# Experts run only on the rows routed to them, in gathered blocks of 128, and gelu by ScalarE's own function

## The chip, the cores and the metric

One core of a Trainium2 chip runs the whole program. The metric is the device time of one execution in microseconds (us). Engines: PE is TensorE, DVE is VectorE, ACT is ScalarE, POOL is GpSimd, SP is SyncE, which only issues DMAs here.

## The reference

x is 16 sequences of 128 rows (the 16 "tiles") with 256 columns. Four stages follow one another, each on a layernorm of x and each added back to x:

- A: attention with 32 query heads of 8 columns over 8 key/value heads, keys and values straight from ctx (128 x 64).
- B: mixture of experts. Each row gets eight sigmoid scores and its two best of 8 experts:

```python
scores = sigmoid(xf @ gate_w.T)
_, sel = top_k(scores + expert_bias, 2)
rin = xf[tok_idx] * sc_sorted[:, None]
for e in range(8):
    h = silu(rin @ w1[e].T) * (rin @ w3[e].T)      # 256 -> 128
    out_sorted += (sorted_exp == e) * (h @ w2[e].T)  # 128 -> 256
routed = zeros.at[tok_idx].add(out_sorted)
shared = (silu(xf @ sw1.T) * (xf @ sw3.T)) @ sw2.T
```

- C: causal attention with 16 heads of 16 columns and projections Wq, Wkv, Wout.
- D: a two-layer network (256 to 1024 to 256) whose weights are rounded to -1, 0, 1 and whose activations are rounded to 8 bits per row, with the tanh form of gelu between the layers.

## The kernel before

Work is cut into parts named by stage and number, and done once for each tile: "B3/5" is part B3 of tile 5. For each engine `PROGRAMS` (lines 82 to 207) is a written list of such words, and `walk` issues them in just that order, so a part that waits holds everything behind it on its engine. Several tiles are under way in different stages at once. Parts hand over by semaphores; TensorE writes into a ring of 4 small (2 KB) and a ring of 2 big (4 KB) PSUM buffers, and a part that fills one first waits for the reader of the buffer's earlier use (`fill`).

Stage A per tile: A1 transposes the normalised tile, ScalarE copies it out, GpSimd splits it into three bf16 parts (`split`), SyncE stores these to DRAM and reads them back as stacked rows of QA (A1r). A2 makes scores once for their maximum (VectorE `neg_max`, line 1149), A3 carries the maximum back as two more rows, A4 makes the scores again transposed, ScalarE exponentiates them, A5 multiplies with the values, A6 transposes and scales. Stage C has the same shape, with projections in front and a causal mask by GpSimd (line 1052).

Stage B per tile: B1 transposes; B2 makes the shared expert and the gate scores; ScalarE takes the exp of the scores, VectorE ranks the eight experts of a row in some ten small operations (lines 1188 to 1206). B3 and B4 (lines 636 to 640) multiply the whole tile with the w1 and w3 of four experts each; ScalarE takes tanh per expert with the row's score as scale, VectorE multiplies (`products`, line 1213), and GpSimd multiplies with a coefficient that is zero for the six experts not chosen (`weigh`, line 1040). B5 transposes the nine hidden tiles, B6 (line 651) sums nine products with w2.

Stage D per tile: DX quantises, D1 transposes, D2 makes 1024 columns, VectorE scales them to z; then the gelu is made by hand: ScalarE squares z (line 908), VectorE (line 1254), ScalarE tanh (line 913), VectorE (line 1260). Its result is quantised (line 1136, 917, 1268), D3 transposes, D4 multiplies and GpSimd adds to x.

At the start SyncE loads the first tiles and the constant rows of KA and KC, whose semaphore `stacks_set` TensorE awaits before its first instruction; ScalarE issues all weight loads. K splits the keys of A in four chunks; SyncE reads each back into KA. S1 and S2 round the weights of D. rstd of every norm is a pow on GpSimd (line 977).

## Time and profile before

| | us |
|---|---|
| median of 3 runs | 653.4 (653.2 to 656.77) |
| the profiled execution's own time | 653.34 |
| its span in the profile | 651.6 |
| TensorE busy | 526.5 |
| VectorE busy | 455.4 |
| ScalarE busy | 296.3 |
| GpSimd busy | 290.8 |
| mean granted TensorE clock, share of full | 0.941 |

The profile is of one execution. The time outside the span is 1.7 us. "Busy" counts an engine's instructions, overlaps once; issuing a DMA, loading a register and waiting are not counted. A float32 product is recorded as two passes, so its group has twice as many entries as the code has calls. The tables hold the rows on which the later argument rests; a group of the view by line tells first the line, engine and operation, then what is written from what, the shapes, the number, and then busy time, mean duration in ns of one, and idle time in front of them with what ended it.

### The profile page before, as it was taken

What the parts mean: (1) busy time and instruction counts of PE and PEld (TensorE: products, weight loads), DVE (VectorE), ACT (ScalarE), POOL (GpSimd) and SP (SyncE); (2) the same over time, 40 slices, a digit from 0 to 9 for tenths busy, and PEclk for the clock granted to TensorE, in tenths of its full rate; (3) what the DMA queues carried; (4) which work ended last, traced back from release to release, by engine and by line L of the source; (5) the groups of instructions that cost most, each with busy time, mean ns of one, the idle gap of its engine ahead of it and who ended that gap; (6) DMA issues with size and microseconds to landing.
All of it is one profiled execution on the core that took longest, in us unless ns stands there. A gap on an engine that the chain in (4) does not pass through costs nothing.

```text
span 651.6 us, 11302 instructions
## 1 busy us (share of the span) xinstructions
PE 526.5 (81%) x3800; PEld 326.5 (50%) x3816; DVE 455.4 (70%) x929; ACT 296.3 (45%) x563; POOL 290.8 (45%) x516
## 2 busy tenths in 40 slices
PE   0035598799999999999999999999999999885651
PEld 0022254355656565656565656565656475564421
DVE  1017848666686878787888877787777777857763
ACT  0122143444446464646454545565555575344332
POOL 5462233445627363636363635353535354456210
PEclk9999788799999999999999998999898999998675
DMA  8642541313140404040404040504040303022000
GB/s 254 178 112 57 139 110 27 85 22 81 31 97 28 105 25 108 26 108 25 108 20 114 16 109 4 121 5 109 4 107 6 81 4 82 24 61 82 2 17 8
DMA packets 82105, 43.96 MB, mean 67 GB/s; under 512 B 48832, under 2 KB 77888, under 8 KB 82048
## 3 DMA queue, kind: packets, MB, share of 16 engines
q1 hardware_dynamic: 78336, 37.98, 23.8%
q10 hardware_dynamic: 3712, 5.26, 2.5%
q8 instruction: 31, 0.51, 0.3%
q14 instruction: 26, 0.21, 0.1%
HBM read 30.42 MB, written 12.32 MB: 66 GB/s over the span
## 4 chain that ended last, share of the span: by engine, by line
PE 56%; DVE 16%; POOL 10%; issue 8%; ACT 5%; DMA 3%; SPq 2%; POOLq 0%; ACTq 0%; DVEq 0%
PE big L625 17%; PE small L605 5%; PE small L562 3%; ACT PC L826 3%; PE big L593 3%; DVE neg_maxA L1149 3%; PE small L655 2%; PE small L613 2%; PE small L648 2%; POOL PC L1052 2%; POOL x L1030 2%; PE small L675 2%; PE big L578 2%; PE small L735 2%; PE small L766 2%
## 5 line engine op out<-in xcount | busy, mean ns | idle before, releaser
L1149 DVE TENSOR_REDUCE neg_maxA<-big 128x8 f32<-128x1024 f32 x64 | 76.7, 1214 | 19.9 <-PE big L578 19.9
L856 ACT ACTIVATE tB<-big,route_half 128x128 f32<-128x128 f32 x128 | 36.5, 368 | 93.2 <-PE big L625 93.2
L1044 POOL TENSOR_TENSOR vB<-vB,route_c 128x512 f32<-128x512 f32 x32 | 33.3, 1040 | 98.9 <-DVE vB L1217 98.9
L826 ACT ACTIVATE PA<-big 128x1024 f32<-128x1024 f32 x64 | 64.7, 1025 | 23.8 <-PE big L593 23.6
L625 PE MATMUL big<-w1T,xTB 128*128 128x512 f32 x128 | 64.6, 628 | 2.9 <-DVE vB L1210 2.7
L655 PE MATMUL small<-w2T,hTB 128*128 128x256 f32 x288 | 65.9, 383 | 0.6 <-ACT hTB L871 0.6
L1052 POOL TENSOR_SCALAR_AFFINE_SELECT PC<-PC 128x1024 f32<-128x1024 f32 x32 | 35.2, 1105 | 56.9 <-ACT PC L826 56.9
L625 PE MATMUL big<-w3T,xTB 128*128 128x512 f32 x128 | 60.5, 595 | 0.0
L655 PEld LDWEIGHTS small<-w2T,hTB 128*128 128x128 f32 x288 | 53.5, 190 | 7.8 <-ACT hTB L871 1.1
L826 ACT ACTIVATE PC<-big 128x1024 f32<-128x1024 f32 x32 | 32.4, 1024 | 21.9 <-PE big L707 21.9
L1175 DVE SCALAR_TENSOR_TENSOR tB<-tB,big 128x512 f32<-128x512 f32 (+1 forms) x48 | 26.4, 550 | 21.4 <-ACT tB L856 21.2
L625 PEld LDWEIGHTS big<-w3T,xTB 128*128 128x128 f32 x128 | 24.6, 193 | 31.3 <-issue 31.3
L1149 DVE TENSOR_REDUCE neg_maxC<-big 128x8 f32<-128x1024 f32 x32 | 38.1, 1216 | 2.2 <-PE big L692 2.1
L625 PEld LDWEIGHTS big<-w1T,xTB 128*128 128x128 f32 x128 | 22.7, 196 | 31.3 <-issue 17.2
L578 PE MATMUL big<-KA,QA 48*128 48x128 bf16 x512 | 26.0, 225 | 14.6 <-DMA QA<-parts_qA 9.1
L562 PE MATMUL small<-ident,xnA 128*128 128x128 f32 x32 | 8.2, 344 | 35.4 <-DMA KC<-onesb 21.8
L605 PE MATMUL small<-PA,VA 128*32 128x512 f32 x256 | 36.4, 653 | 0.0
L593 PE MATMUL big<-QA,KA 50*128 50x512 bf16 x128 | 25.1, 402 | 8.5 <-DVE neg_maxA L1149 3.9
L688 PE MATMUL big<-mask,identb 128*128 128x512 bf16 x64 | 26.5, 414 | 6.3 <-ACT PC L826 4.2
L838 ACT ACTIVATE OA<-small 128x512 f32<-128x512 f32 x32 | 19.1, 597 | 25.6 <-PE small L605 25.5
L578 PEld LDWEIGHTS big<-KA,QA 48*128 48x128 bf16 x512 | 15.2, 97 | 26.1 <-DMA QA<-parts_qA 10.5
L692 PE MATMUL big<-KC,QC 96*128 96x128 bf16 x256 | 27.1, 232 | 0.0
(171 smaller groups left out, 1213.7 us busy)
## 6 DMA issues: line engine op xcount, KB each, us to landing
parts_qA<-QP SPq DMA_DIRECT2D x16, 192.0 KB, 3.0
QA<-parts_qA SPq DMA_DIRECT2D x32, 96.0 KB
parts_kC<-KPC SPq DMA_DIRECT2D x16, 192.0 KB, 2.1
KC<-parts_kC SPq DMA_DIRECT2D x16, 192.0 KB, 3.1
parts_qC<-QPC SPq DMA_DIRECT2D x16, 192.0 KB, 2.4
QC<-parts_qC SPq DMA_DIRECT2D x16, 192.0 KB, 2.9
x<-in_x SPq DMA_DIRECT2D x16, 128.0 KB, 3.0
QA<-parts_qA SPq DMA_DIRECT2D x32, 64.0 KB
```

The source lines that it names most:

```text
L562: last = transpose(dst[:, c * P:(c + 1) * P], src[:, c * P:(c + 1) * P], idn[:])
L578: last = mm(ps[:, c * BANK + g * P:c * BANK + (g + 1) * P], QA[u][rows, G0 * j + g, :], KA[rows, j, t * P:(t + 1) * P], start=True, stop=True)
L593: last = mm(ps[:, c * BANK:(c + 1) * BANK], KA[rows, j, t * P:(t + 1) * P], QA[u][rows, G0 * j:G0 * (j + 1), :], start=True, stop=True)
L605: last = mm(ps[SLOT * j:SLOT * (j + 1), :], VA[u][:, kv, :], PA[:, kv * G0:(kv + 1) * G0, :], start=True, stop=True)
L625: last = mm(ps[:, o:o + n], xTB[:, c, :], w[c], start=(c == 0), stop=(c == DC - 1))
L655: last = mm(ps[:, 0:D], hTB[:, e, :], w_2[:, e, :], start=(e == 0), stop=(e == NE - 1))
L692: last = mm(ps[:, b * BANK + i * P:b * BANK + (i + 1) * P], QC[u][0:K1, h, :], KC[u][0:K1, h, :], start=False, stop=(i == 3))
L826: return op(dst[:, 8 * j:8 * (j + 1), :], ps[:].rearrange("p (h t) -> p h t", t=P), ACT.Exp, scale=scale).then_inc(S[name], 1)
L856: ins = op(tB[:, (e0 + i) * HID:(e0 + i + 1) * HID], ps[:, i * HID:(i + 1) * HID], ACT.Tanh, scale=rt["half"][:, e0 + i:e0 + i + 1])
L1044: g.tensor_tensor(hB[:, sl].rearrange("p (e h) -> p e h", e=4), vB[:, sl].rearrange("p (e h) -> p e h", e=4), rt["c"][:, e0:e0 + 4].unsque ...
L1052: g.affine_select(out=p, in_=p, compare_op=ALU.is_ge, fill=0.0, base=0, pattern=[[0, 8], [1, P]], channel_multiplier=-1).then_inc(S["PC_ca ...
L1149: v.tensor_reduce(dst[:, 8 * j:8 * (j + 1)], ps[:].rearrange("p (h t) -> p h t", t=P), FREE, ALU.max, negate=True).then_inc(S[name], 1)
```

## The change

The tiles are taken through stage B in batches of 4, 8 and 4. Each tile still goes through the shared expert and the gate (B1, B2, B5, B6), now with one product of 264 columns for both sides. BX stores its normalised rows to DRAM. For four tiles at a time R ranks the experts; R2 counts, by a product with a triangle of ones, how many rows before a row chose the same expert, which gives the place of each (row, choice) in a table sorted by expert. SC scatters the entries (row number, half score, half squared score) there by indirect DMA, two for each tile. `plan` works out where each block of 128 places begins and whose expert it is. A batch of n tiles has 2n + 7 blocks, so 15, 23 and 15, whatever the routing.

For a block, MB loads a register and 128 entries, MG gathers 128 rows of x by indirect DMA, M1 transposes them, M2 multiplies with w1 and w3 of the one expert whose column is in a register, M3 transposes the hidden tile, M4 multiplies with w2, MY stores 128 result rows. YG gathers the two result rows of each row by indirect DMA, and CY adds them to x. Buffers: 3 for gathered rows, 2 for each later step.

The gelu is one ScalarE activation (`Gelu_apprx_tanh`) from z to g2. D1's copy moves from VectorE to ScalarE. The first bf16 part of a split is written by ScalarE out of PSUM, and not by GpSimd. EPS is added by VectorE. The constant rows are awaited where they are used; the weights are issued in three portions, the later ones after the first KA and QA; the reads of KA move to ScalarE's queue; the rounding of the weights of D borrows PC, so that C6/0 waits for it. All five written orders are new; a stretch of TensorE's shows how blocks stand between parts of other tiles. The diff, cut:

```diff
-GROUPS = ((8, 1), (0, 4), (4, 4))
+BATCHES = ((0, 4), (4, 8), (12, 4))
+RT = 4
+MOST = max(n for _, n in BATCHES)
+NB = 2 * MOST + E - 1
+BLOCKS = tuple((2 * t0 + i * (E - 1), 2 * n + E - 1) for i, (t0, n) in enumerate(BATCHES))
...
+        M3/22 M3/23 D4/3 M2/24 M2/25 M4/22 M4/23 M1/26 M1/27 M3/24 M3/25 A5.0/13 M2/26 M2/27 M4/24 M4/25 M1/28 M1/29
...
+    rows_x = [nc.dram_tensor(f"rows_x{i}", (n * P, D), F32).ap() for i, (_, n) in enumerate(BATCHES)]
+    table = [nc.dram_tensor(f"table{i}", (places(n), 4), F32).ap() for i, (_, n) in enumerate(BATCHES)]
+    rows_y = [nc.dram_tensor(f"rows_y{i}", (n * P, D), F32).ap() for i, (_, n) in enumerate(BLOCKS)]
...
-            sp.wait_ge(S["onesb"], 1)
-            for c in range(2):
-                sp.dma_start(KA[c * HALF + K0:c * HALF + K0 + 2, :, :], onesb[:]).then_inc(S["stacks_set"], 16)
-            for x in KC:
-                sp.dma_start(x[K1:KM, :, :], onesb[0:2 * H1, :]).then_inc(S["stacks_set"], 16)
...
+                sp.wait_ge(S["zeros_set"], 1)
+                for x in table:
+                    sp.dma_start(x.rearrange("(p n) w -> p (n w)", p=P), zeros[:, 0:x.shape[0] * 4 // P]).then_inc(S["zeros_in"], 16)
...
+                i = block_of(b)[0]
+                n = BATCHES[i][1]
+                s.wait("plan", i)
+                sp.wait_ge(table_in[i], 16 * 2 * n)
+                if b >= NQ:
+                    sp.wait_ge(ent_in[b % NQ], 16 * (b // NQ))
+                place0 = sp.value_load(row_of[0:1, b:b + 1], min_val=0, max_val=places(n) - P)
+                sp.dma_start(entB[:, b, :], table[i][bass.ds(place0, P), :]).then_inc(ent_in[b % NQ], 16)
+            def MY(s, b, u):
+                s.wait("yM", b)
+                i, k = block_of(b)
+                sp.dma_start(rows_y[i][k * P:(k + 1) * P, :], yM[u][:]).then_inc(S[f"rows_in{u}"], 16)
...
+            def M1(s, b, u):
+                pe.wait_ge(xg_in[b % NG], 16 * (b // NG + 1))
+                turn(s, xg[b % NG], ident)
+                cols[b] = pe.value_load(col_of[0:1, b:b + 1], min_val=0, max_val=(E - 1) * D)
+
+            def M2(s, b, u):
+                if b == 0:
+                    pe.wait_ge(w_in["M"], 16 * (DC + 1))
+                s.wait("xgT", b)
+                ps, full = s.fill()
+                for c in range(DC):
+                    last = mm(ps[:, 0:2 * HID], xgT[u][:, c, :], w_13[:, c, bass.ds(cols[b], 2 * HID)], start=(c == 0), stop=(c == DC - 1))
+                last.then_inc(full, 1)
+
+            def M3(s, b, u):
+                s.wait("hM", b)
+                ps, full = s.fill()
+                transpose(ps[:, 0:P], hM[u][:], ident[:]).then_inc(full, 1)
+
+            def M4(s, b, u):
+                s.wait("hMT", b)
+                ps, full = s.fill()
+                mm(ps[:, 0:D], hMT[u][:], w_2[:, bass.ds(cols[b], D)], start=True, stop=True).then_inc(full, 1)
...
+                    for c in range(DC):
+                        act.dma_start(w_q[:, c, :], a["WqT"][c]).then_inc(w_in["C"], 16)
+                        act.dma_start(w_o[:, c, :], a["WoutT"][c]).then_inc(w_in["C"], 16)
+                    for c in range(DC):
+                        act.dma_start(w_13[:, c, :], a["w13T"][c]).then_inc(w_in["M"], 16)
+                    act.dma_start(w_2[:, 0:E * D], a["w2T"].rearrange("e h d -> h e d")).then_inc(w_in["M"], 16)
+
+            def Kr(s, t, u):
+                i = t
+                act.wait_ge(S["kpA_out"], 16 * (i + 1))
+                for c in range(2):
+                    for row, n in STACK:
+                        act.dma_start(KA[c * HALF + row * HD0:c * HALF + (row + n) * HD0, :, i * KCHUNK * P:(i + 1) * KCHUNK * P],
+                                     parts_kA[i][3 - n:3, c]).then_inc(KA_in[i], 16)
...
+            def M2(s, b, u):
+                ps = s.read()
+                act.wait_ge(ent_in[b % NQ], 16 * (b // NQ + 1))
+                s.before("hMT", b - 1)
+                op(hM[u][:], ps[:, 0:HID], ACT.Tanh, scale=entB[:, b, 1:2]).then_inc(S["tM"], 1)
...
-                op(zz, z, ACT.Square, scale=2.0 * 0.044715 ** 0.5).then_inc(S["zz"], 1)
-
-            def D2b(s, t, u):
-                s.wait("inner", t)
-                s.before("g2", t)
-                op(th, inner, ACT.Tanh, scale=2.0 * (2.0 / np.pi) ** 0.5).then_inc(S["th"], 1)
+                s.before("gq", t)
+                op(g2[:], z, ACT.Gelu_apprx_tanh).then_inc(S["g"], 1)
...
+            def SC(s, t, u):
+                if t == 0:
+                    pool.wait_ge(S["zeros_in"], 16 * 2)
+                i = batch_of(t)
+                s.wait("entry", t // RT)
+                s.wait("place", t // RT)
+                for k in range(2):
+                    g.indirect_dma_start(table[i], at(place[:, t, k:k + 1]), entry[:, t, k, :], None).then_inc(table_in[i], 16)
+
+            def MG(s, b, u):
+                i = block_of(b)[0]
+                for k in range(2):
+                    pool.wait_ge(S[f"rows_out{k}"], 16 * (sum(BATCHES[i]) // 2))
+                pool.wait_ge(ent_in[b % NQ], 16 * (b // NQ + 1))
+                s.before("xgT", b - NG + 1)
+                g.indirect_dma_start(xg[b % NG][:], None, rows_x[i], at(entB[:, b, 0:1].bitcast(I32))).then_inc(xg_in[b % NG], 16)
+
+            def YG(s, t, u):
+                i = batch_of(t)
+                for k in range(2):
+                    pool.wait_ge(S[f"rows_in{k}"], 16 * rows_returned(i, k))
+                s.wait("row", i)
+                s.before("x2_done", t - 1)
+                for k in range(2):
+                    g.indirect_dma_start(yg[k][u][:], None, rows_y[i], at(row[:, t, k:k + 1])).then_inc(S[f"yg_in{u}"], 16)
 
...
+            def M2(s, b, u):
+                ps = s.read()
+                s.wait("tM", b)
+                chain(s, b, v.scalar_tensor_tensor(out=hM[u][:], in0=hM[u][:], scalar=1.0, in1=ps[:, 0:HID], op0=ALU.add, op1=ALU.mult))
+                v.scalar_tensor_tensor(out=hM[u][:], in0=hM[u][:], scalar=entB[:, b, 2:3], in1=ps[:, HID:2 * HID], op0=ALU.mult,
+                                       op1=ALU.mult).then_inc(S["hM"], 1)
...
+            def CY(s, t, u):
+                s.landed("yg_in", t, 2)
+                s.wait("shared", t)
+                chain(s, t, v.tensor_tensor(X[:, t, :], X[:, t, :], yg[0][u][:], ALU.add))
+                v.tensor_tensor(X[:, t, :], X[:, t, :], yg[1][u][:], ALU.add).then_inc(S["x2_done"], 1)
```

In the VectorE program `R` has 16 operations on four tiles at once, `R2` 5, `plan` 11 and `returned` 5, the last two once a batch.

## Rows read from the trace of the kernel before

**Rows 1.** The page: busy us, share of the span and number of instructions of each engine
```profile
PE 526.5 (81%) x3800; PEld 326.5 (50%) x3816; DVE 455.4 (70%) x929; ACT 296.3 (45%) x563; POOL 290.8 (45%) x516
```
**Rows 2.** Stretches: length, busy time of PE, PEld, DVE, ACT, POOL, then PEclk
```profile
0.00:100.00 100.00, 41.47 (x204) 22.33 (x205) 40.74 (x64) 19.71 (x36) 40.61 (x85) 0.91 0.52 138
100.00:600.00 500.00, 462.42 (x3418) 289.88 (x3431) 384.42 (x816) 259.40 (x508) 240.21 (x418) 0.98 0.24 59
600.00:651.60 51.60, 22.61 (x181) 14.26 (x181) 30.19 (x51) 17.19 (x19) 10.03 (x13) 0.65 0.03 11
...
560.00:600.00 40.00, 31.86 (x230) 23.78 (x233) 27.36 (x62) 18.44 (x38) 21.15 (x34) 0.96 0.23 64
```
**Rows 3.** Chain of waits, first 90 us: start, duration, what
```profile
10.33 11.17 DMA KC<-onesb
...
43.15 4.00 DMA QA<-parts_qA
```
**Rows 4.** Instructions in order of time, 632 to 652 us: start, duration, engine, line
```profile
633.24 0.72 POOL L1057 TENSOR_TENSOR x<-x,y 128x256 f32<-128x256 f32 x1 [4.84 <-DVE y L1274]
...
648.69 0.72 POOL L1057 TENSOR_TENSOR x<-x,y 128x256 f32<-128x256 f32 x1 [14.73 <-DVE y L1274]
```
**Rows 5.** Groups by line, PE, whole span: the expert products and their transposes
```profile
L655 PE MATMUL small<-w2T,hTB 128*128 128x256 f32 x288 | 65.9, 383 | 0.6 <-ACT hTB L871 0.6
...
L625 PE MATMUL big<-w1T,xTB 128*128 128x512 f32 x128 | 64.6, 628 | 2.9 <-DVE vB L1210 2.7
L625 PE MATMUL big<-w3T,xTB 128*128 128x512 f32 x128 | 60.5, 595 | 0.0
...
L648 PE MATMUL small<-ident,vB 128*128 128x128 f32 x144 | 22.6, 280 | 0.7 <-POOL vB L1044 0.7
...
L625 PE MATMUL big<-sw1T_gateT,xTB 128*128 128x136 f32 x64 | 12.6, 323 | 0.7 <-issue 0.5 <-ACT PA L826 0.2
...
L625 PE MATMUL big<-sw3T,xTB 128*128 128x128 f32 x64 | 10.6, 293 | 0.0
```
**Rows 6.** The same, PE: two passes like those of a block
```profile
L735 PE MATMUL small<-WoutT,oTC 128*128 128x256 f32 x64 | 17.2, 392 | 1.9 <-ACT oTC L903 1.9
...
L562 PE MATMUL small<-ident,xnC 128*128 128x128 f32 x32 | 6.7, 292 | 0.0
```
**Rows 7.** The same, DVE: gating, routing (first and last of 11 groups), gelu
```profile
L1260 DVE SCALAR_TENSOR_TENSOR g<-th,z 128x1024 f32<-128x1024 f32 x16 | 23.3, 1455 | 2.3 <-ACT th L913 1.6
...
L1217 DVE TENSOR_TENSOR vB<-tB,big 128x512 f32<-128x512 f32 x32 | 22.0, 687 | 1.1
...
L1254 DVE SCALAR_TENSOR_TENSOR th<-z 128x1024 f32<-128x1024 f32 x16 | 19.8, 1239 | 3.1 <-ACT z L908 3.1
...
L1198 DVE TENSOR_TENSOR gt<-route_v 128x64 f32<-128x64 f32 x16 | 6.8, 427 | 0.6
...
L1194 DVE TENSOR_TENSOR route_v<-route_score,bias 128x8 f32<-128x8 f32 x16 | 2.5, 155 | 0.0
```
**Rows 8.** The same, ACT: expert tanh, the gelu's square, table load
```profile
L856 ACT ACTIVATE tB<-big,route_half 128x128 f32<-128x128 f32 x128 | 36.5, 368 | 93.2 <-PE big L625 93.2
...
L908 ACT ACTIVATE z<-z 128x1024 f32<-128x1024 f32 x16 | 17.0, 1060 | 12.2 <-DVE z L1249 11.5
...
L811 ACT ACT_TABLE_LOAD x1 | 1.3, 1283 | 22.5 <-PE small L562 22.5
```
**Rows 9.** The same, POOL; then its end of the first K split, in time
```profile
L1044 POOL TENSOR_TENSOR vB<-vB,route_c 128x512 f32<-128x512 f32 x32 | 33.3, 1040 | 98.9 <-DVE vB L1217 98.9
...
7.94 1.15 POOL L986 TENSOR_TENSOR PC<-gT,PC 64x512 bf16<-64x512 f32 x1
```
**Rows 10.** DMAs: six issues in a row, in time; then a landing (KB, us)
```profile
34.51 4.32 SPq L466 DMA_DIRECT2D KA<-parts_kA  x6
...
x<-in_x SPq DMA_DIRECT2D x16, 128.0 KB, 3.0
```
**Rows 11.** In order of time: a weight load of PE that waits for issue alone
```profile
617.27 0.15 PEld L766 LDWEIGHTS small<-f2q,gT 128*128 128x128 bf16 x1 [0.28 <-issue]
```

706 lines of the change are left out of this document (416 added, 290 removed), and 4 rows, old and new, of the table PARTS.

## The prediction

> **What bounds the kernel now.** I began with the busy shares [rows 1]: TensorE works 526.5 of 651.6 us, VectorE 455.4, ScalarE and GpSimd under 300 each. A share alone says little, so I cut the span in three [rows 2]. From 100 to 600 us TensorE is busy 462.4 of 500 us, 92.5%, while VectorE has 77%: there TensorE is the bound, and only 37.6 us of it are idle. In the first 100 us it idles 58.5 us and in the last 51.6 us 29.0 us. Idle time adds up to 125.1 us, so the span is 526.5 of work plus three pieces of idleness, and I forecast each piece apart.
>
> The chain of waits says why the start is empty [rows 3]: TensorE's first transpose waits to 21.5 us for the constant rows of KC, stuck behind the weight loads, and the first score products wait to 47.2 us for QA. The end is stage D of the last tile, one operation after another; its result comes 15.5 us after that of the tile before, 648.69 against 633.24 [rows 4].
>
> **TensorE's work.** The groups by line [rows 5] price what goes. All-expert products w1T and w3T: 64.6 + 60.5 = 125.1 us. Of w2T eight ninths: 65.9 x 8/9 = 58.6. Of the transposes of hB eight ninths: 22.6 x 8/9 = 20.1. Together 203.8 us. The shared expert's two products (12.6 + 10.6) become one of 264 columns; at 0.229 us for 256 columns (65.9/288) and 0.489 for 512 (62.6/128), its 64 passes cost 15.2, which saves 8.
>
> What comes is 15 + 23 + 15 = 53 blocks, a fixed number, however the rows are routed: the 4,096 routed rows would fill 32 full ones, the other 21 are padding. One block is two transposes, four passes of 256 columns, one transpose, two passes. By the dearest like rows [rows 6], 0.21 and 0.269 us, that is 3 x 0.21 + 6 x 0.269 = 2.25 us; by the cheapest, 22.6/144 = 0.157 and 0.229, it is 1.85. I take 2.05, 109 us in all (98 to 119). The counting products (R2) are some 40 short ones, about 2 us. So 526.5 - 203.8 - 8 + 109 + 2 = 426 us.
>
> **The other engines.** VectorE [rows 7] loses two gating passes at 22.0, eleven routing groups between 6.8 and 2.5 us each (45.3 in all), 19.8 and 23.3 of the hand-made gelu and 4.6 for yT: 137. It gains 106 short operations in the blocks at 0.28 (30), 132 of routing and planning at about 0.35, between the 0.166 of the shortest and 0.427 of the longest row (46), 64 additions of EPS at 0.15 (10) and 32 additions of gathered rows at 0.42 (13). 455 - 137 + 99 = 417 us, practically TensorE's load.
>
> ScalarE [rows 8] loses 36.5 of tanh, 17.0 each for square and second tanh and 17 of copies, 88; it gains 16 gelus at 1.06 (17), the yT copies (6), 48 second copies at 0.385 (18) and per block a tanh at 0.368 and three copies, 1.43 (76): 325 us. The trace shows one table load, 1.28 us, for Exp, Tanh, Square and Copy together. Gelu is new in it. In the new ScalarE order Gelu and Exp change places 21 times; if each costs such a load, that is 27 us more, if none, nothing. ScalarE has room for either, so I put nothing on the path for it; a rival below prices the other case. The Trainium skill (ScalarE: Activation LUTs, "Table sets: the hidden batching unit") has one expensive anchor to a set and lists gelu apart from exp. By that rule the 27 us come, and by its figure of 2.66 us with the drain they are an estimated 56.
>
> GpSimd [rows 9] loses 33.3 of weighing and 40 of variance scaling and casts: 218 us stay. It gains 117 indirect DMAs (32 scatters, 53 gathers of blocks, 32 returns). The trace has none. Below stand the 4.32/6 = 0.72 us of SyncE's plain issues in a row, above the 3.0 that a transfer of x needs to land [rows 10]. With 128 addresses to work out I take 1.2, nearer to the issue: 140, sum 358 us.
>
> Each block also loads a register on TensorE (the expert's column), of which the trace has nothing. The nearest is a weight load that waits 0.28 us for issue alone [rows 11]; a gain is excluded, since nothing is taken away for it; above, the 3.0 us landing. I take 0.28: 53 x 0.28 = 15 us. SyncE issues 16 normalised tiles, 53 entries, 53 results and 3 zero fills more and 24 K reads less: 101 at 0.72, 73 us over the whole run. Behind an entry load that waits for the plan stand the QA and QC loads of later tiles; I count that as covered by their lead of two buffers, and where it is not, A2 or C4 starts late, which is in the fill below.
>
> The change adds waits too. ScalarE's second copies wait for the store of two tiles earlier and its copy of a block's result for the store of two blocks earlier. A store lands in about 3.0 us [rows 10] and a pair of blocks takes over 4, so I cost them at nothing; if they were late, the exps queued behind them, and TensorE with them, would be too.
>
> **Idle time of TensorE after.** Start: the constant rows, the weights and the split on GpSimd leave the head. K's split ended at 9.1 us on GpSimd even before [rows 9]; the store lands in about 4.0 [rows 3], six issues take 4.32 [rows 10], their landing 4.0 again: products from about 22 us instead of 47.2, and 58.5 - 25 = 34. The f1 scales move behind the first products but stay in VectorE's sum. The 24 reads of K go from SyncE to ScalarE's queue, 17 us at 0.72, in a stretch where ScalarE is busy 19.7 of 100 us [rows 2]; if that cover fails, the first four QA copies are late by as much.
>
> Middle: the 426 us less about 41 in the first 100 us and 33 after the middle, as before or a little more [rows 2], so 352 us of work. Before it was filled to 92.5%, with one dominant engine. Now two engines carry 426 and 417 in written orders, and a batch of four stops at its routing: 16 ranking operations (5.6), 5 for the places (1.8), eight scatters (9.6) and their landing (3.0), an entry load (3.7), a gather (4.2), so 28 us from the last gate to the first block, which only stage A of later tiles covers. The nearest row is 560 to 600 us, where the stages begin to run out: 31.9 of 40, 80% [rows 2]. I take 82%: 352/0.82 - 352 = 77 idle.
>
> End: 29.0, less 2.5 (gelu's square and tanh at 1.06 and VectorE's two passes, 23.3/16 and 19.8/16 at most [rows 7], become one of 1.06, about 3.6 saved; a table load of 1.28 [rows 8] may take part of it back). But the last batch gives its four tiles back together, and stages C and D of all four run out then, two by two. Each pair costs at least one gap of 15.5 us [rows 4]; I add between one and two, 22: 29.0 - 2.5 + 22 = 48.
>
> Sum: 426 + 34 + 77 + 48 + 15 = 600, and 1.7 outside the span gives 602. The profiled execution took 653.3, the median is 653.4, so no correction between them.
>
> **Rivals.**
> A: it packs as densely as before. For it: ScalarE and GpSimd had 45% and each batch is interleaved with stage A, C and D of other tiles. The middle at 92.5% idles 28 instead of 77: 553 us. Against it: VectorE no longer has slack.
> B: blocks run at the pace of their own chain. One block is 0.42 + 0.39 + 1.08 + 0.37 + 0.57 + 0.21 + 0.29 + 0.54 + 0.39 = 4.3 us in ten links, with handovers about 5; two stand in the buffers, so 2.5 a block, and with late gathers or registers at 1 us, 3.0 or more against 2.2 assumed. 53 x 0.8 = +43: 645. TensorE would idle there and its clock with it: it was granted 0.65 in the last stretch, where it was 44% busy, against 0.98 in the middle [rows 2]. Against: the orders pair blocks so that four are between stages.
> C, slower: GpSimd becomes the bound. The place is its in-order queue, where the rsqrt of all four norms, the splits and the masks stand behind indirect DMAs. Its work is 218 + 117x; at 90% filled, with 34 ahead and 20 behind, it passes 660 us from x = 2.8. At 3.0 it gives 569/0.9 + 54 = 686. For it: an instruction on 128 computed addresses has no row; against: the plain landing of 3.0 includes transfer, for which the queue does not wait. The Trainium skill (SBUF — State Buffer, "SBUF: two separate sides") warns that a DMA issued by GpSimd starves of descriptors while VectorE holds the shared port, and gives 620 ns that become 3100; by that figure an estimated 581/0.9 + 54 = 699. No row here shows it.
> D: the 21 table loads lie on the path, at most places in the end and in front of the exps: 602 + 22 = 624.
>
> **Chances.** Forecast 0.42, A 0.20, B 0.17, D 0.08, C 0.11, and 0.02 that gains and new waits cancel. The range 550 to 668 holds the forecast, B, D and most of A and leaves C out: the two outer halves are under 2 in 10. A measurement can tell about 1% from no change. Faster by over 1%: 0.42 + 0.20 + 0.08 + 0.15 of B = 0.85; within 1%: 0.03; slower: 0.12.
>
> **What would show it.** TensorE's busy time 415 to 440; below 400 or above 460 the block price is wrong. First products of A2 before 25 us, or the head is not what I took it for. VectorE's busy time within 10 us of TensorE's. The middle's fill: 82% mine, over 90% A. Idle of TensorE inside the blocks named "issue" gives the register's price; idle named VectorE or ScalarE in a block gives B; GpSimd busy or issuing over 80% and rsqrt as the common releaser gives C; table loads counted on ScalarE and their place on the chain give D. The forecast fails if the indirect DMA costs over 2.8 us, if a register load costs over 1.4, or if the run-out of the last four tiles idles TensorE by more than 90 us.

## The result, and the profile after

The changed kernel takes **697.9 us** (median; 694.5 to 700.3) against 655.1 (653.2 to 657.0) for the kernel before, run beside it: ratio **1.065**, 95% interval 1.059 to 1.070. I had forecast 602. It is slower, and not through the mechanism that my slower rival named. One execution, of kernel 15 below, ran at a lower granted clock than its like (0.687 against 0.758 to 0.761) and is left out of that kernel's median.

The page of the changed kernel, the same view as [rows 1] of the kernel before: busy us, share of the span and number of instructions of each engine.

```profile
PE 479.9 (69%) x3614; PEld 307.7 (44%) x3625; DVE 420.5 (61%) x965; ACT 339.2 (49%) x684; POOL 331.1 (48%) x502
```

TensorE has 46.6 us less work, but the span, 692.5, is 40.9 longer: idle time of TensorE went from 125.1 to 212.6 us. The stretches say where it lies; [rows 2] has those of before.

The changed kernel in stretches: start:end, length, busy time (instructions) of PE, PEld, DVE, ACT, POOL, then PEclk, DMA share, GB/s.

```profile
0.00:100.00 100.00, 41.91 (x251) 20.29 (x252) 46.12 (x77) 24.47 (x43) 41.70 (x93) 0.91 0.56 152
100.00:600.00 500.00, 385.93 (x2924) 252.88 (x2931) 327.90 (x796) 274.04 (x587) 265.38 (x372) 0.90 0.37 92
...
600.00:692.50 92.50, 52.05 (x440) 34.50 (x442) 46.43 (x93) 40.73 (x54) 23.98 (x38) 0.75 0.13 39
```

The first 100 us are as full as before (41.9 against 41.5), the middle is busy 77% where it was 92.5%, and the last stretch is 92.5 us long. The granted clock in the middle fell from 0.98 to 0.90.

The prices of what came, in groups by line (the view of [rows 5] to [rows 9]): out<-in, count | busy us, mean ns | idle before and its releasers.

```profile
L789 PE MATMUL small<-w13T,xgT 128*128 x212 | 62.4, 433 | 8.4 <-ACT xgT L1023 5.0 <-ACT VC L1056 1.5 <-DVE hM L1477 0.9
L1232 POOL DMA_INDIRECT xg<-rows_x,entB x53 | 51.7, 976 | 71.8 <-ACT xgT L1023 54.0 <-DMA entB<-table 10.5 <-issue 7.2
...
L800 PE MATMUL small<-w2T,hMT 128*128 x106 | 32.1, 403 | 3.5 <-ACT hMT L1034 1.8 <-issue 1.0 <-ACT xgT L1023 0.5
L1241 POOL DMA_INDIRECT yg<-rows_y,row x32 | 31.7, 990 | 15.1 <-issue 6.7 <-DMA rows_y<-yM 4.6 <-DVE x L1484 3.5
...
L745 PE MATMUL small<-sw1T_gateT_sw3T,xTB 128*128 128x264 f32 x64 | 21.6, 469 | 0.5 <-ACT xTB L1007 0.4
L679 PE MATMUL small<-ident,xg 128*128 128x128 f32 x106 | 21.5, 287 | 9.9 <-DVE hM L1477 6.0 <-DMA xg<-rows_x,entB 3.5 <-ACT OC L1069 0.2
...
L1476 DVE SCALAR_TENSOR_TENSOR hM<-hM,small 128x128 f32<-128x128 f32 x53 | 15.2, 286 | 62.2 <-ACT hM L1029 62.2
L1085 ACT ACT_TABLE_LOAD x11 | 14.1, 1283 | 0.2
L795 PE MATMUL small<-ident,hM 128*128 128x128 f32 x53 | 13.9, 293 | 5.8 <-DVE hM L1477 2.9 <-issue 2.2 <-ACT yM L1040 0.7
...
L990 ACT ACT_TABLE_LOAD x10 | 12.8, 1283 | 0.5 <-PE big L853 0.3
```

The blocks take TensorE 62.4 + 32.1 + 21.5 + 13.9 = 129.9 us, 2.45 each. An indirect DMA holds GpSimd for 0.98 us. VectorE sits 62.2 us waiting for a block's tanh.

TensorE's largest waits in the changed kernel: us in total, times, longest.

```profile
PE big L695 <- DMA QA<-parts_qA: 32.0, 8, 14.2
PE small L679 <- DVE xnA L1312: 22.0, 3, 11.2
```

Named waits are small and many; no single one holds the 87 us of new idleness. So I marked progress instead. GpSimd adds the first attention's result to x once for each tile, and stage D's result once for each tile. When these additions run says how far the two halves have come. They are the next fences: engine, operation, shortest/median/longest ns, first and last start in us. Kernel before, then after:

```profile
L1030 POOL TENSOR_TENSOR x<-x,oA x16: 722/741/1692, 76.5 to 551.2; 128x256 f32<-128x256 f32 x16
L1057 POOL TENSOR_TENSOR x<-x,y x16: 721/724/822, 203.6 to 648.7; 128x256 f32<-128x256 f32 x16
```

The same view of the changed kernel:

```profile
L1212 POOL TENSOR_TENSOR x<-x,oA x16: 712/728/767, 67.4 to 449.2; 128x256 f32<-128x256 f32 x16
L1251 POOL TENSOR_TENSOR x<-x,y x16: 722/731/1222, 286.2 to 682.6; 128x256 f32<-128x256 f32 x16
```

Before, the first attention advances one tile in (551.2 - 76.5)/15 = 31.6 us, stage D follows in step, and 97.5 us after the last tile's attention all is done. After, attention advances faster, 25.5 us a tile, and is through 102 us earlier; but the second attention and stage D may start on a tile only when its whole batch has returned, and 233.4 us are left to do then. The batches turned an even flow into two halves. Two halves alone are not the loss, though: kernel 3 below has them too, in the same written order without the blocks, and is faster than the kernel before.

### The profile page after: what moved, and what is told of

The parts are those of the page before. It is cut to its first block, busy times and chain, and to the rows that moved or that the text cites. A ratio compares the mean times of both kernels' runs of the same rounds, so it can differ in the third digit from the quotient of the medians.

```text
span 692.5 us, 12270 instructions
## 1 busy us (share of the span) xinstructions
PE 479.9 (69%) x3614; PEld 307.7 (44%) x3625; DVE 420.5 (61%) x965; ACT 339.2 (49%) x684; POOL 331.1 (48%) x502
## 4 chain that ended last, share of the span: by engine, by line
PE 26%; DVE 17%; issue 13%; POOL 12%; DMA 11%; ACT 10%; SPq 8%; ACTq 1%; POOLq 0%; DVEq 0%
PE small L789 5%; SPq L578 4%; POOL table L1224 3%; ACT PA L990 3%; PE small L862 2%; DMA parts_kA<-PC 2%; PE small L679 2%; DVE neg_maxC L1344 2%; PE big L895 2%; POOL PC L1246 2%; DMA xg<-rows_x,entB 2%; PE small L800 2%; DMA QA<-parts_qA 2%; POOL yg L1241 1%; DVE neg_maxA L1344 1%
## 5 line engine op out<-in xcount | busy, mean ns | idle before, releaser
L1344 DVE TENSOR_REDUCE neg_maxA<-big 128x8 f32<-128x1024 f32 x64 | 76.2, 1215 | 26.2 <-PE big L695 25.2
L1232 POOL DMA_INDIRECT xg<-rows_x,entB x53 | 51.7, 976 | 71.8 <-ACT xgT L1023 54.0
L789 PE MATMUL small<-w13T,xgT 128*128 x212 | 62.4, 433 | 8.4 <-ACT xgT L1023 5.0
L1476 DVE SCALAR_TENSOR_TENSOR hM<-hM,small 128x128 f32<-128x128 f32 x53 | 15.2, 286 | 62.2 <-ACT hM L1029 62.2
L789 PEld LDWEIGHTS small<-w13T,xgT 128*128 128x128 f32 x212 | 43.0, 214 | 20.0 <-issue 14.0
L1224 POOL DMA_INDIRECT table<-entry,place x32 | 31.7, 991 | 20.6 <-DVE place L1432 10.8
L1241 POOL DMA_INDIRECT yg<-rows_y,row x32 | 31.7, 990 | 15.1 <-issue 6.7
L1029 ACT ACTIVATE hM<-small,entB 128x128 f32<-128x128 f32 x53 | 19.4, 369 | 35.5 <-PE small L789 32.9
L800 PE MATMUL small<-w2T,hMT 128*128 x106 | 32.1, 403 | 3.5 <-ACT hMT L1034 1.8
L853 PE MATMUL big<-QC,KC 98*128 98x128 bf16 x256 | 22.1, 244 | 9.2 <-DMA QC<-neg_maxT_C 5.2
L679 PE MATMUL small<-ident,xg 128*128 128x128 f32 x106 | 21.5, 287 | 9.9 <-DVE hM L1477 6.0
L1501 DVE SCALAR_TENSOR_TENSOR z<-big,qscale,f_scale 128x1024 f32<-128x1024 f32 x16 | 20.5, 1284 | 12.7 <-PE big L895 12.4
```

The source lines that it names most:

```text
L679: last = transpose(dst[:, c * P:(c + 1) * P], src[:, c * P:(c + 1) * P], idn[:])
L789: last = mm(ps[:, 0:2 * HID], xgT[u][:, c, :], w_13[:, c, bass.ds(cols[b], 2 * HID)], start=(c == 0), stop=(c == DC - 1))
L800: mm(ps[:, 0:D], hMT[u][:], w_2[:, bass.ds(cols[b], D)], start=True, stop=True).then_inc(full, 1)
L1224: g.indirect_dma_start(table[i], at(place[:, t, k:k + 1]), entry[:, t, k, :], None).then_inc(table_in[i], 16)
L1232: g.indirect_dma_start(xg[b % NG][:], None, rows_x[i], at(entB[:, b, 0:1].bitcast(I32))).then_inc(xg_in[b % NG], 16)
L1241: g.indirect_dma_start(yg[k][u][:], None, rows_y[i], at(row[:, t, k:k + 1])).then_inc(S[f"yg_in{u}"], 16)
```

## The experiments

Each ran beside the kernel before, whose medians were 654.1 to 655.2; ratios are to it, with 95% intervals. Two kernels that are set against each other here may come from different sessions: the kernel before moved by 1.1 us between them, and the changed kernel's own four executions lie 5.8 us apart, so differences of a few us say nothing. "..." marks lines left out of an edit. "Programs" are the written orders of the five engines.

**1. Are the table loads on the path (rival D)?** One function exchanged, so that this kernel leaves out the gelu:

```diff
-                op(g2[:], z, ACT.Gelu_apprx_tanh).then_inc(S["g"], 1)
+                op(g2[:], z, ACT.Tanh).then_inc(S["g"], 1)
```

> The changed kernel with Tanh in place of Gelu in D2 (the gelu is left out; Tanh needs no other table). Theory T, the table loads cost the time: the 21 changes between Gelu and Exp, 1.28 us each and more with what waits for them, lie on the path, and without them the kernel takes about 670 to 680 us instead of 698. Theories B (the blocks cost more than priced) and S (the new order and head cost it): 690 us or more, within 8 us of the changed kernel.

Measured 698.3, ratio 1.066 (1.063 to 1.068). ScalarE's busy time fell from 339.2 to 311.7, by the 21 loads; the time did not move. D falls.

**2. How much do blocks cost?** 32 blocks instead of 53 (the rows of 21 are left out):

```diff
-NB = 2 * MOST + E - 1
+NB = 2 * MOST
-BLOCKS = tuple((2 * t0 + i * (E - 1), 2 * n + E - 1) for i, (t0, n) in enumerate(BATCHES))
+BLOCKS = tuple((2 * t0, 2 * n) for i, (t0, n) in enumerate(BATCHES))
...
```

> The changed kernel with 8, 16 and 8 blocks instead of 15, 23 and 15, so that 21 are left out (rows whose block is left out get another row's result). Theory B1, a block costs its work on TensorE, 2.35 us in this trace (1.03 + 0.67 + 0.38 + 0.27): 21 x 2.35 = 49 less, 649 us. Theory B2, a block costs its pace, the 52 us that the first 15 take, 3.5 us each: 74 less, 624 us. Theory S, blocks stand beside other work and cost little at the margin: 680 us or more.

Measured 684.5, ratio 1.045 (1.042 to 1.049): 13 us for 21 blocks, 0.64 each.

**3. No blocks at all** (ranking, plan and scatters stay; the blocks, the gathers of their results and so the routed experts' result are left out):

```diff
 programs, all engines:
-MB/* MG/* MY/* M1/* M2/* M3/* M4/* YG/*
```

> The changed kernel without any block and without the gathers of results (routed experts left out; ranking, planning and the scatters stay, the two additions stay on buffers of zeros). Theory B1: 53 x 2.35 = 125 less, 573 us. Theory B2: 53 x 3.5 = 186 less, 512 us. Theory S: more than 600 us, since what is slow is the rest.

Measured 630.1, ratio 0.961 (0.958 to 0.964). All blocks together, with the gathers of their results, cost 68 us: the first 32 blocks 54 of them (684.5 against 630.1), 1.7 each, the other 21 only 13. Neither of my two prices per block (2.35 and 3.5) fits; both kernels came out above the bounds of theory S.

**4. The same taken from the kernel before**: its routed experts' products, 204 us of TensorE, are left out; gating and routing stay.

```diff
 programs:
-B3/* B4/* B5.1/* B5.2/*
-                for e in range(NE):
-                    last = mm(ps[:, 0:D], hTB[:, e, :], w_2[:, e, :], start=(e == 0), stop=(e == NE - 1))
+                last = mm(ps[:, 0:D], hTB[:, E, :], w_2[:, E, :], start=True, stop=True)
...
```

> The kernel before without its routed experts (B3, B4, their transposes and eight of nine products of B6 left out; ranking stays). TensorE has 204 us less work, VectorE 411 us of work then becomes the bound: 490 to 530 us. Theory S, the new order, head and routing cost time: at least 40 us below the changed kernel without blocks. Theories B1 and B2: within 15 us of it, and the whole loss is in the blocks.

Measured **664.5, ratio 1.014** (1.011 to 1.017). This is the run that breaks my forecast: taking away the largest piece of the busiest engine's work made the kernel 9 us slower, where I had expected 490 to 530. Its page:

```profile
PE 401.5 (61%) x3160; PEld 241.0 (36%) x3176; DVE 413.1 (62%) x865; ACT 246.3 (37%) x403; POOL 257.4 (39%) x484
```

Its middle stretch, columns as above:

```profile
100.00:600.00 500.00, 337.05 (x2768) 202.19 (x2780) 339.00 (x740) 208.08 (x353) 203.20 (x379) 0.78 0.23 56
```

526.5 - 203.8 should have left 323 us of TensorE's work; 401.5 are there. The granted clock in the middle is 0.78 where it was 0.98, and the steps that stayed are longer. The attention's products with V, before and in this kernel:

```profile
L605 PE MATMUL small<-PA,VA 128*32 128x512 f32 x256 | 36.4, 653 | 0.0
```

```profile
L591 PE MATMUL small<-PA,VA 128*32 128x512 f32 x256 | 50.8, 890 | 0.0
```

The rest of the freed time became waits, whose longest are (us in total, times, longest):

```profile
POOL PC L1037 <- ACT PC L811: 148.5, 19, 13.7
...
PE small L548 <- DVE yq L1130: 71.0, 14, 6.1
```

**5. Is it the clock?** Kernel 4 with products that nothing reads, where TensorE waits for D1 and A3:

```diff
+                ps, full = s.fill()
+                idle_work(ps, 16)          # 8 ahead of A3's wait
                 s.wait("yq", t)
...
```

> The kernel before without its routed experts (left out, as in before_0), with idle products put where TensorE waits longest there: 16 of 512 columns ahead of D1's wait, 8 ahead of A3's. Theory K, the clock took the gain back (granted 0.776, 401 us busy where the groups that stay come to 322 at the clock of before): the idle products raise the granted clock above 0.85 and the time falls below 645 us although TensorE is given work. Theory L, a loop of waits through VectorE, ScalarE, GpSimd and the transfers sets the pace and the clock does not matter: 660 to 690 us, no better than 664.

Measured 650.1, ratio 0.994 (0.991 to 0.998): 14 us **faster** than kernel 4 with 52 us more on TensorE (453.6 busy), at a clock of 0.889 in place of 0.776. The products with V came down with it:

```profile
L596 PE MATMUL small<-PA,VA 128*32 128x512 f32 x256 | 40.6, 722 | 0.0
```

So the lower clock is part of why kernel 4 gains nothing: work that only raised the clock made the kernel faster. The time lies between my two expectations (below 645, or 660 to 690): even with most of the clock back it is within 1% of the kernel before. I put the rest down to waits between the engines; that is argued from what is left over, and the wait was not found.

**6. Is GpSimd's in-order queue the block's limit?** It waits 54.0 us for xgT in front of gathers. More gather buffers:

```diff
-NG, NQ = 3, 4
+NG, NQ = 5, 4
```

> The changed kernel with 5 buffers for gathered rows instead of 3, so that GpSimd's gathers wait less for the copy of an earlier block (54 us of such waits in the trace). Theory C, GpSimd's in-order queue behind these waits holds the rest up: at least 10 us faster, below 688. Theory K or S: within 5 us of 698.

Measured 702.5, ratio 1.071 (1.067 to 1.076). The wait fell from 54.0 to 16.1 us, and no time was won.

**7. Do the expert weights, 3 MB early on ScalarE's queue, clog the head?**

```diff
 program of ScalarE:
-Kr/3
+Kr/3 WM/0        # WM: the loads of w13T and w2T, which stood ahead of Kr/1
```

> The changed kernel with the 3 MB of expert weights issued behind the last read of KA instead of ahead of the second. Theory H, the head's gain was lost to these weights (the second group of six KA reads takes 13.79 us to issue, QA waits up to 14.2 us): 10 to 20 us faster, 678 to 688. Rival: the head's time is set by the scales of f1 and f2, by GpSimd and by VectorE, and moving them saves under 4 us.

Measured 703.5, ratio 1.076 (1.070 to 1.083). The weights do clog the head: the second six reads of KA, which took ScalarE's queue 13.79 us in the changed kernel, take 4.87 here (start, duration, operation), and the first addition comes at 61.8 us instead of 67.4. But the end does not come earlier for it.

```profile
30.87 4.87 ACTq L954 DMA_DIRECT2D KA<-parts_kA  x6
```

**8. The other half of the change alone**: the gelu function in the kernel before.

```diff
-                op(zz, z, ACT.Square, scale=2.0 * 0.044715 ** 0.5).then_inc(S["zz"], 1)
-                op(th, inner, ACT.Tanh, scale=2.0 * (2.0 / np.pi) ** 0.5).then_inc(S["th"], 1)
+                op(g2[:], z, ACT.Gelu_apprx_tanh).then_inc(S["th"], 1)
...
```

> The kernel before with only the gelu changed to ScalarE's own function (VectorE loses 43 us of work, ScalarE 17, but Gelu and Exp alternate in every tile, up to 32 table loads of 1.28 us, 41 us). Theory L or K, the pace of the middle is a chain, not TensorE's work: it may move by the shorter chain of stage D, 5 to 15 us faster. Theory T: the loads stand in front of the exps of A and C and it gets slower, 665 to 690. By my prediction's ledger, with TensorE as the bound: 3 us faster, from the end alone.

Measured 657.4, ratio 1.004 (1.002 to 1.007). VectorE's busy time fell by 44.8 us to 410.6, and no time was won: 0.4% more, where I had expected 5 to 15 us less by one theory, 3 less by another, and 665 to 690 by the third.

**9, 10. Does the loop pass through stage D?** Stage D written one tile later, in kernel 4 and in the changed kernel.

```diff
 programs, all engines:
-D*/t where it stood
+D*/(t-1) there, D*/15 at the end
```

> The kernel before without its routed experts, with every part of stage D taken one tile later in all five written orders (D of tile k where D of tile k + 1 stood, the last tile's at the end). Theory L, the written order makes a loop of waits that passes through stage D (TensorE waits 71 us for yq): with a tile more of lead the middle runs faster, below 640 us against 664, although the end gets some 15 us longer. Rival, the loop does not pass through D: 670 to 685 us, the longer end alone.

> The changed kernel with stage D one tile later in all orders. Theory L: TensorE's 13 us on yq, 8 on gq and VectorE's 12 on z go, 5 to 20 us faster (680 to 693). Rival: the order was already loose there and the longer end shows, 700 to 715 us.

Measured 674.8, ratio 1.032 (1.030 to 1.035), and 726.7, ratio 1.111 (1.107 to 1.116). The additions of kernel 9 run from 77.2 to 554.0, 31.8 us a tile against 32.3 in kernel 4; what is left after the last attention grew from 96.9 us to 115.5. A tile of slack in front of D is worth half a us a tile, so the pace is not set by a loop through D.

**11. Idle work in the changed kernel**, 277 products ahead of A2, D1 and M3:

```diff
+                idle_work(ps, 8)           # A2.0; 6 ahead of D1, 1 ahead of M3
```

> The changed kernel with idle products of 512 columns where TensorE waits: 8 ahead of A2/0's wait, 6 ahead of D1's, 1 ahead of M3's, 277 in all, some 60 us at full clock. Theory K, the clock (granted 0.88 against 0.94) costs time here too: granted 0.92 or more and the time stays or falls by up to 15 us in spite of the work given. Rival: TensorE's work is what counts in this order and the time rises by 20 us or more.

Measured 725.6, ratio 1.109 (1.104 to 1.113), clock 0.87. TensorE's busy time rose by 58.1 us, to 538.0, and the time by 27.8: about half of the given work went into idle time, the rest lengthened the kernel, and the clock did not rise (0.88 in the changed kernel). I take its idle pieces to be too short and scattered for more.

**12. The head of the change alone**, in the kernel before:

```diff
+            def O(s, t, u):        # KC's constant rows, after C0/3, awaited by C6
+                for x in KC:
+                    sp.dma_start(x[K1:KM, :, :], onesb[0:2 * H1, :]).then_inc(S["stacksC_set"], 16)
...
-            pe.wait_ge(S["stacks_set"], 16 * 4)
 program of ScalarE: the weight loads after A1/1
```

> The kernel before with the start of the change alone: the constant rows awaited where they are used (KC's later in SyncE's order) and the large weight loads issued by ScalarE behind A1/1. Theory H: TensorE's first work moves from 21.7 to about 8 us and everything follows, 8 to 18 us faster, 637 to 647, which would beat both kernels. Rival: the K splits, QA and the scales of f1 set the first 80 us in any case: within 4 us of 655.

Measured 653.7, ratio 0.999 (0.996 to 1.003). TensorE's first transpose came at 6.3 us instead of 21.5, and the first addition at 76.2, as before (76.5).

**13. Do the blocks wait for their gathers?** All 53 gathers left out, hand-overs kept:

```diff
 program of GpSimd:
-MG/*
-                pe.wait_ge(xg_in[b % NG], 16 * (b // NG + 1))
...
```

> The changed kernel without its 53 indirect gathers of rows: each block takes whatever stands in its buffer (set to zero once), so the blocks compute nothing useful, with all their other steps, table loads from memory and register loads in place. Theory L (the blocks cost time through their four hand-overs between TensorE, ScalarE and VectorE and the slots that they take in the written order of all engines): at least 690. Rival G (a block waits for its gather: GpSimd's 0.98 us of issue and some 3 us of landing, 53 times, stand on the path, as does GpSimd's wait for xgT of 54 us in all): back by most of the 54 to 68 us that the blocks cost, 640 to 660.

Measured 697.2, ratio 1.065 (1.056 to 1.073): the gathers cost nothing.

**14. Idle work in kernel 3**, 8 products ahead of A2, 6 ahead of D1:

```diff
+                idle_work(ps, 8)           # A2.0; 6 ahead of D1
```

> The kernel of after_0 (changed kernel without blocks and result gathers) with products that nothing reads ahead of two of TensorE's waits: 8 ahead of the first attention's scores, 6 ahead of the transposes of yq, 224 in all. Theory K (without the experts' work the clock falls, 0.811 there against 0.941 before, and that stretches what is left, as in before_0_fill, where idle work gave 14 us back): the clock goes to 0.87 or more and the time falls below 625. Rival W (in this order the idle time of TensorE is scattered in short pieces, so that given work costs more than the clock returns, as in after_fill): above 635.

Measured 635.9, ratio 0.969 (0.962 to 0.976), clock 0.827 in place of 0.811: 42.8 us more on TensorE than kernel 3, and 5.7 us more time, with ratios whose intervals overlap. Theory K falls, and rival W's bound of 635 is just passed: in the new order these products brought neither the clock back nor any time.

**15, 16. Does the loop pass through stage C?** Stages C and D one tile later, in kernel 4 and in the whole kernel before:

```diff
 programs, all engines:
-C*/t D*/t where they stood
+C*/(t-1) D*/(t-1) there, C*/15 D*/15 at the end
```

> The kernel of before_0 (kernel before without its routed experts' work on TensorE, 664.5) with the second attention and the last stage written one tile later in all five programs, so that what stage C hands to the next tile's stage A has a tile more of slack. Theory O (the period of 33 to 34 us per tile is a loop through stage C and the next tiles' first attention in the written order; after_0, whose order keeps them further apart, is 34 us faster): the stretch from 200 to 500 us carries more tiles, a period under 32.5 us, and with one tile of C and D more at the end (15 to 20 us) 635 to 660 in all. Rival N (the period is set inside one stage or by the clock, the order does not matter): same period, 675 to 685.

> The kernel before, with all of its computation, with the second attention and the last stage written one tile later in all five programs. Theory O (the order of the stages sets the pace with the experts too): 630 to 655. Rival B (with the 204 us of expert work in it TensorE is near enough to full that the order gives nothing, and the longer end comes on top): 665 to 680.

Measured 712.2, ratio 1.088 (1.081 to 1.096), and 712.1, ratio 1.085 (1.078 to 1.092), far above both ranges that I had given for either. The additions of kernel 16:

```profile
L1027 POOL TENSOR_TENSOR x<-x,oA x16: 723/743/1694, 77.9 to 546.9; 128x256 f32<-128x256 f32 x16
L1054 POOL TENSOR_TENSOR x<-x,y x16: 722/726/732, 237.3 to 706.5; 128x256 f32<-128x256 f32 x16
```

31.3 us a tile against 31.6 before, and 31.6 against 32.3 in the other pair: theory O falls, a tile more of slack hardly speeds the flow. What it costs is the end, 159.6 us after the last attention instead of 97.5, three to four times what I had allowed for it. And again it makes no difference whether the 204 us of expert products are there (712.1) or not (712.2).

**17. Do the hand-overs inside a burst of blocks pace it?** The chain of waits of the changed kernel in its first burst (start, duration, what), from one row product (L789) to a later one:

```profile
167.31 0.88 PE small L789 x4
...
169.49 0.41 PE small L679 x2
169.90 0.49 issue
170.39 0.67 PE small L800 x2
171.06 0.88 PE small L789 x4
```

Row product, tanh and two gating steps (in the lines left out), transposes, last product (L800), the next row product: 171.06 - 167.31 = 3.75 us for a block of 2.45. This is the slow step of two: the row product before stood at 165.28 and the one at 167.14 followed it within 1.86 us. Over the burst it is 42.3/14 = 3.0 us a block, by the copies of the results shown below. So I wrote other blocks' steps into these waits:

```diff
 programs of TensorE, ScalarE, SyncE:
-M3/b, M4/b and MY/b where they stood
+M3/(b-1), M4/(b-2) and MY/(b-2) there, the last ones at the batch's end
-        hM = two("hM", [P, HID])
+        hM = [sb(f"hM_{i}", [P, HID]) for i in range(3)]      # hMT too
```

> The changed kernel, all of its computation kept, with the third step of a block written one block later and the fourth two blocks later, in the programs of TensorE, ScalarE and SyncE, and three buffers for hM and hMT where there were two. Theory L (a block costs 3.4 to 3.9 us in a batch's burst because each one's steps wait for each other: 0.88 of the second step, 1.2 of ScalarE and VectorE on hM, 0.41 of the transposes, 0.5 until hMT is there, 0.67 of the fourth step; the waits between them have no other block's work written into them): a block comes down towards its 2.45 us of TensorE, up to 1 us for each of 53, 650 to 675. Rival S (the slots that the blocks take in the written order of the engines cost the time, whatever the depth inside the burst): 690 or more.

Measured 715.3, ratio 1.094 (1.090 to 1.098). ScalarE's copies of the blocks' results in three bursts, in the changed kernel and in this one (first and last start):

```profile
L1040 ACT ACTIVATE yM<-small x15: 377/384/415, 159.1 to 201.4; 128x256 f32<-128x256 f32 x15
L1040 ACT ACTIVATE yM<-small x23: 378/384/401, 346.0 to 409.7; 128x256 f32<-128x256 f32 x23
L1040 ACT ACTIVATE yM<-small x15: 357/384/465, 500.6 to 562.7; 128x256 f32<-128x256 f32 x15
```

```profile
L1035 ACT ACTIVATE yM<-small x15: 377/384/390, 167.9 to 208.2; 128x256 f32<-128x256 f32 x15
L1035 ACT ACTIVATE yM<-small x23: 377/384/401, 369.2 to 427.4; 128x256 f32<-128x256 f32 x23
L1035 ACT ACTIVATE yM<-small x15: 364/384/415, 534.0 to 584.0; 128x256 f32<-128x256 f32 x15
```

The bursts did get shorter, 42.3 to 40.3, 63.7 to 58.2, 62.1 to 50.0, and what stands between them got longer by more. In the chain of kernel 17 the next wait had taken the place of the one removed, a gather that lands late:

```profile
385.88 4.26 DMA xg<-rows_x,entB
...
390.19 0.44 PE small L674 x2
```

**18. Does TensorE's own work in the blocks lie on the path?** One of the two transposes and one of the two halves of the row product are left out of each block:

```diff
-                for c in range(DC):
-                    last = mm(ps[:, 0:2 * HID], xgT[u][:, c, :], w_13[:, c, bass.ds(cols[b], 2 * HID)], start=(c == 0), stop=(c == DC - 1))
+                last = mm(ps[:, 0:2 * HID], xgT[u][:, 0, :], w_13[:, 0, bass.ds(cols[b], 2 * HID)], start=True, stop=True)
...
```

> The changed kernel with half of the first and second step's products of each block left out (one of the two transposes and one of the two halves of the row product, so that the blocks' values are wrong), every hand-over kept: some 0.65 us less of TensorE in each of 53 blocks, 34 us in all. Theory L in the form that what TensorE does in a block lies on the block's own chain as well: 665 to 680. Rival W (only waits for other engines pace the blocks, TensorE's work in them is covered): 690 or more.

Measured 704.7, ratio 1.078 (1.075 to 1.082): less work and no less time, as by rival W. TensorE's busy time fell by 5 us only where some 34 were taken away, at a clock of 0.846 in place of 0.88.

**Where the blocks' 68 us lie** the additions of kernel 3 show (63.6 of them in the two profiled spans, 692.5 and 628.9):

```profile
L1175 POOL TENSOR_TENSOR x<-x,oA x16: 721/728/757, 68.3 to 397.9; 128x256 f32<-128x256 f32 x16
L1214 POOL TENSOR_TENSOR x<-x,y x16: 719/726/1100, 265.6 to 625.3; 128x256 f32<-128x256 f32 x16
```

The last attention is at 397.9 there and at 449.2 with blocks, 51 us later; from then on the two need 227.4 and 233.4. So 38 blocks of the first two bursts cost 51 us, and the 15 of the third, which have stages C and D of other tiles written between them, 6; another 6 come after the last addition (692.5 - 682.6 against 628.9 - 625.3). These last 6 are no work of a block: they are GpSimd's closing DRAIN, the instruction on which its program ends, in the changed kernel and in kernel 3:

```profile
L308 POOLq DRAIN  x1: 9750/9750/9750, 682.5 to 682.5; - x1
```

```profile
L270 POOLq DRAIN  x1: 3460/3460/3460, 625.2 to 625.2; - x1
```

It takes 0.82 us in the kernel before, which has no indirect DMA, 3.46 with 32 (kernel 3), 6.08 with 64 (kernel 13), 8.69 with 96 (kernel 2) and 9.75 with 117. In the changed kernel SyncE has seen the last store land at 685.04, and the span ends at 692.5, after this DRAIN: some 7 of the 41 us that the span grew are this term, for which the forecast had nothing. That it grows with their number is read from these kernels; no run changed it alone.

One stretch inside the second burst, in the changed kernel and in kernel 3:

```profile
350.00:400.00 50.00, 39.75 (x200) 28.89 (x200) 15.19 (x41) 31.46 (x77) 16.68 (x18) 0.93 0.46 112
```

```profile
350.00:400.00 50.00, 35.83 (x242) 20.44 (x242) 32.87 (x83) 19.72 (x46) 16.20 (x29) 0.86 0.16 42
```

VectorE, the engine that the attention needs most, does 15 us of work in these 50 instead of 33.

## Why the prediction was wrong

**The step that failed** is the first one: "there TensorE is the bound, and only 37.6 us of it are idle", and with it "the span is 526.5 of work plus three pieces of idleness", from which the removed products were taken at their full length. I read 92.5% busy as a limit, and priced 204 us of removed products at 204 us. Kernel 4 shows their worth in this kernel: less than nothing (+9 us). The pace, 31.6 us a tile with the products, is 32.3 without. The busy share was high because expert products stood in the written order where TensorE would otherwise have waited, and they held the clock up besides (0.98 in the middle with them, 0.78 without). Neither is visible in a busy share. The chain of waits of the kernel before, in which TensorE had 56%, would not have told either; what tells is leaving the work out.

**Piece by piece**, against the profiled 692.5 (forecast 600 before the 1.7 outside the span):

| term | forecast | measured |
|---|---|---|
| TensorE's work | 426 | 479.9 |
| idle, first 100 us | 34 | 58.1 |
| idle, 100 to 600 us | 77 | 114.1 |
| idle, after 600 us | 48 | 40.5 |
| register loads | 15 | 5.5, within the rows above |
| GpSimd's closing DRAIN | nothing | 7, within the row after 600 us |

- *Registers.* A read was dearer than the 0.28 that I took: with the arithmetic behind it, it held TensorE's queue for 0.59 us in the median, 33.6 us in all. But it ran mostly behind products still under way; TensorE stood idle in 5.5 us of it, added up from the trace. The 0.49 us of "issue" in the chain of experiment 17 are such a read. The price was too low and the cover, for which the forecast had nothing, made up for it.

```profile
L781 PEldq TENSOR_LOAD <-col_of x53: 295/303/697, 151.4 to 549.7; - x53
```

- *Work, +54.* Blocks 129.9 instead of 109, since a pass cost 0.294 to 0.303 us (62.4/212, 32.1/106) and not 0.269 at most; the merged shared product 21.6 instead of 15.2. The other 27 are nearly all steps that the forecast took over unchanged and that lasted longer at a clock of 0.88 (the products with V 0.721 us in place of 0.653): the range of 415 to 440 supposed the old clock. By its own sign, above 460, the block price was wrong, and that is 21 of the 54.
- *Head, +24.* The first transposes came at 11 us instead of 21.5 and the first products of A2 at 28.7 instead of 47.2 (the forecast's sign was before 25), and TensorE idled as long in the first 100 us as before: K's reads, moved to ScalarE's queue, stood in front of the first qTA and kTC. One piece of the chain of waits of the changed kernel there:

```profile
18.89 9.05 DMA KA<-parts_kA
```

ScalarE in order of time, same kernel: start, duration, operation, [idle before <- releaser].

```profile
32.24 13.79 ACTq L956 DMA_DIRECT2D KA<-parts_kA  x6
46.08 0.38 ACT L1052 ACTIVATE kTC<-small 128x256 f32<-128x256 f32 x1 [16.52 <-DMA parts_kA<-PC]
```

  I had priced these reads at 0.72 each in a free queue; the second six took 13.8, and with the weight loads issued before them they kept ScalarE from its next copy for 16.5. Behind the loads of the expert weights they were not in a free queue: with those moved away the six take 4.87 (kernel 7). A landing that I had put at 4.0 took 9.05. I named this cover as the one that might fail, and put nothing for it in the sum. But the head is not what was lost: kernel 7 has a better one and no better time, and kernel 12 the same in the old order.
- *Middle, +37.* Fill 77% and not 82%. The gap from the last gate to the first block was not covered: in the 48 us before the first burst TensorE works 33.2, 69%, where the kernel before had 41.4. In the three bursts it is fuller, 82 to 86%; 84 of the 114 us of idleness lie outside them. The stretches before and in the first burst, and the one behind the second, columns as above:

```profile
100.00:148.00 48.00, 33.17 (x253) 15.29 (x252) 38.37 (x89) 21.30 (x40) 19.61 (x25) 0.82 0.20 41
148.00:201.00 53.00, 43.80 (x265) 30.00 (x265) 26.58 (x70) 27.55 (x82) 24.04 (x34) 0.97 0.49 111
...
410.00:500.00 90.00, 63.80 (x497) 42.32 (x499) 61.54 (x159) 43.42 (x90) 64.51 (x90) 0.89 0.32 84
```

- *End, -8*, but "after 600" now holds more than the run-out, and some 7 us of GpSimd's DRAIN; near by luck.
- *VectorE 420.5* (417 forecast) and *ScalarE 339.2* (325 and 27 for the loads) came as worked out, GpSimd 331.1 for 358 since an indirect DMA costs 0.98 and not 1.2. Counting the work of these three was not the weak side of the forecast. VectorE did not come within 10 us of TensorE, which went up instead.
- *Small slips.* The chain of a block in rival B has nine links and not ten (the sum of 4.3 stands); the 3.0 that I gave a store is the row of a load, and the blocks' stores landed in 1.8.
- None of the three things by which the forecast was to fail came: an indirect DMA at 2.8 us, a register load at 1.4, a run-out of 90 us of idleness. The list had no line for the bound itself.

**The rivals.** C, the only slower one, had the sign for a wrong reason: it needed 2.8 us for an indirect DMA, and 0.98 were measured; without the 53 gathers the time is the same (kernel 13). The Trainium skill (SBUF — State Buffer, "SBUF: two separate sides") has a GpSimd-issued DMA go from about 620 to about 3100 ns beside a VectorE copy that holds the shared port; in this trace, with VectorE 61% busy, the longest of 117 held GpSimd for 1.48 us. Whether any of VectorE's instructions here took the port in that way, the trace does not say. D: the 21 loads came, 14.1 + 12.8 us, at 1.28 us each, and cost no time (kernel 1). The Trainium skill (ScalarE: Activation LUTs, "What ACT_TABLE_LOAD costs") has about 1283 ns for the load, which the trace shows to the ns, and 2.66 us with a drain; but 20 of the 21 start 0.02 us after the instruction before them ends, and in 18 the next instruction starts within 0.03 us of the load's end, so that no drain shows. B was nearest: in the first two bursts a block runs at 3.0 and 2.9 us, slower than its 2.45 of work, and B gave 3.0 or more with late gathers or dear registers. But its price, 0.8 us for each of 53 on top of 602, rested on the same failed step, and the one edit that loosened that chain (kernel 17) won nothing. A was furthest off.

**What is shown, and what is open.** Shown: the removed products were worth nothing (4, 15 against 16); part of the reason is the clock (5); leaving out the gathers or the table loads, loading the weights later or giving the gathers more buffers wins nothing (13, 1, 7, 6); the blocks cost 68 us (3), 51 of the 64 in the profiled spans before the last attention is through. The account is then a table of two by two:

| | without routed work | with it |
|---|---|---|
| old order | 664.5 | 655.1 |
| new order | 630.1 | 697.9 |

Without the routed work the changed kernel is 34 us ahead. That is the worth of everything else that the change brought, taken together: order, head, gelu, splits and ranking by four tiles; no run takes these apart, though the gelu (8) and the head (12) alone won nothing in the old order. In the old order the old way of computing the experts is free; in the new one the new way costs 68. Open: what sets the 31 to 32 us a tile in the old order. It is not stage D or C of the tile before (9, 15, 16), nor the 45 us of VectorE's gelu (8), nor the expert products. Open too is why the blocks cost what they do: denser bursts (17) and lighter blocks (18) won nothing, and no edit of the blocks that kept all 53 got near 655. That the third burst is cheap because other stages are written between its blocks is read from the trace, and not tried. None of the versions that compute everything beats the kernel before; kernel 12 equals it.
